# Order of work in a mixture of experts: gathers ahead of scatters, routing steps a tile apart, a last weight copy to another place, and twelve unread products

## What is computed

```python
x = _layernorm(x + _L0_attn_ref(x, ...))          # gated linear attention
x = _layernorm(x + _L0_xattn_ref(x, ctx_768, ...)) # 16 heads, 77 context rows
x = _layernorm(x + _L0_ffn_ref(x, ...))            # 8 experts, the best 2 of each token
x = _layernorm(x + _L1_attn_ref(x, ...))
x = _layernorm(x + _L1_xattn_ref(x, ctx_768, ...))
x = _layernorm(x + _L1_ffn_ref(x, ...))

def _L0_ffn_ref(x, Wg, W1, W2, W3):
    ...
    for e in range(E):
        u = jnp.einsum('bsd,dh->bsh', x, W1[e])
        v = jnp.einsum('bsd,dh->bsh', x, W2[e])
        h = u * jax.nn.sigmoid(u) * v
        y = jnp.einsum('bsh,hd->bsd', h, W3[e])
        out = out + y * weights[..., e][..., None]
```

## Time and profile before

| | us |
|---|---|
| median of 3 runs | 1141.53 |
| lowest and highest run | 1140.96, 1144.29 |
| the profiled execution, whole | 1150.01 |
| its span, first to last instruction | 1148.3 |
| PE busy in it | 1013.1 (88%) |
| DVE, ACT, POOL busy | 617.3, 425.2, 255.9 |
| mean granted clock of PE, of its full speed | 0.968 |

### The profile page before, as it was taken

The page is one execution under the profiler, slowest core; times in us unless marked ns, Lnnn a source line. Parts: engine busy times, 40 slices in busy tenths (PEclk is TensorE's granted clock), DMA queues, the critical chain, the costliest instruction groups (busy, mean ns, idle before and its releaser), DMA issues.

```text
span 1148.3 us, 20834 instructions
## 1 busy us (share of the span) xinstructions
PE 1013.1 (88%) x8628; PEld 723.1 (63%) x8628; DVE 617.3 (54%) x1398; ACT 425.2 (37%) x557; POOL 255.9 (22%) x282
## 2 busy tenths in 40 slices
PE   6889889889998898999998798989888987986887
PEld 3666566566565798997445465756556574753656
DVE  2653753753867463333334845665574759755333
ACT  1533533533513445555541244152406323340212
POOL 0310310310210223333332130231103111202642
PEclk9999999999988898999999899999999999997999
DMA  6014313213201971111112000200010010005427
GB/s 186 1 42 149 109 42 125 69 42 121 73 1 32 370 237 37 47 47 47 47 43 92 1 5 2 83 2 6 16 59 2 6 37 1 2 1 152 151 88 233
DMA packets 64238, 80.50 MB, mean 70 GB/s; under 512 B 12736, under 2 KB 57681, under 8 KB 63121
## 3 DMA queue, kind: packets, MB, share of 16 engines
q1 hardware_dynamic: 53392, 61.15, 16.1%
q0 software_dynamic: 5664, 15.47, 4.2%
q10 hardware_dynamic: 5088, 2.56, 0.9%
HBM read 46.13 MB, written 33.03 MB: 69 GB/s over the span
## 4 chain that ended last, share of the span: by engine, by line
PE 44%; issue 21%; DVE 16%; ACT 12%; SPq 2%; DMA 2%; POOL 2%; another core or an unknown queue 1%; ACTq 0%; DVEq 0%; POOLq 0%
PE ps L1511 8%; DVE sb_arena L865 6%; ACT sb_arena L642 6%; PE ps L1647 5%; PE ps L1669 3%; PE ps L1717 3%; PE ps L1772 3%; DVE sb_arena L869 3%; PE ps L1619 2%; PE ps L1983 2%; DVE ps L886 2%; PE ps L1555 1%; SPq L433 1%; PE ps L1998 1%
## 5 line engine op out<-in xcount | busy, mean ns | idle before, releaser
L642 ACT ACTIVATE sb_arena<-ps 77x2048 f32<-77x2048 f32 (+1 forms) x64 | 116.7, 1880 | 28.2 <-PE ps L1601 27.0
L1377 POOL TENSOR_TENSOR sb_arena<-sb_arena,sb_neghalf 128x2 f32<-128x2 f32 x40 | 28.7, 719 | 398.1 <-DVE sb_arena L831 398.1
L1511 PE MATMUL ps<-sb_arena,sb_wreg 128*128 128x256 f32 (+1 forms) x512 | 109.0, 361 | 6.8 <-issue 3.8
L1846 PE MATMUL ps<-sb_arena 128*128 128x128 f32 x800 | 104.4, 287 | 2.4 <-ACT sb_arena L750 2.1
L1846 PEld LDWEIGHTS ps<-sb_arena 128*128 128x128 f32 x800 | 101.2, 203 | 4.5 <-ACT sb_arena L750 2.8
L1511 PEld LDWEIGHTS ps<-sb_arena,sb_wreg 128*128 128x128 f32 (+1 forms) x512 | 88.0, 193 | 23.3 <-issue 8.3
L1619 PE MATMUL ps<-sb_arena 32*77 32x256 f32 (+1 forms) x1024 | 79.4, 428 | 25.3 <-ACT sb_arena L642 12.7
L750 ACT ACTIVATE sb_arena<-sb_arena 128x1024 f32 x72 | 76.0, 1056 | 17.1 <-issue 13.1
L1619 PEld LDWEIGHTS ps<-sb_arena 32*77 32x77 f32 (+1 forms) x1024 | 45.0, 179 | 45.8 <-ACT sb_arena L642 23.7
L865 DVE TENSOR_REDUCE sb_arena<-ps 128x8 f32<-128x2048 f32 x32 | 71.1, 2285 | 3.5 <-PE ps L1575 3.5
L1452 POOL DMA_INDIRECT outs<-sb_arena,sb_idx x36 | 36.3, 1010 | 145.6 <-ACT sb_arena L740 145.6
(11 more groups left out here) (285 smaller groups left out, 1890.4 us busy)
## 6 DMA issues: line engine op xcount, KB each, us to landing
sb_arena<-in_m_w SPq DMA_DIRECT2D x8, 1536.0 KB, 10.7
sent<-sb_xres SPq DMA_DIRECT2D x32, 256.0 KB
sb_arena<-outs SPq DMA_DIRECT2D x16, 512.0 KB, 6.3
outs<-sb_zeros SPq DMA_DIRECT2D x4, 1664.0 KB, 9.8
sent<-sb_zeros SPq DMA_DIRECT2D x2, 2560.0 KB, 13.7
sb_arena<-in_m_w SPq DMA_DIRECT2D x16, 256.0 KB
early<-sb_xres SPq DMA_DIRECT2D x12, 256.0 KB, 2.9
sb_arena<-in_xT SPq DMA_DIRECT2D x8, 256.0 KB, 3.4
```

Of the source, the lines that this page charges most:

```text
L642: nc.scalar.activation(dst, src, ACT.Exp).then_inc(S(f"h_PT{p}"), 1)
L1511: ins = mm(dst[:, m * cols:(m + 1) * cols], wt[0:rows, k, m * P:(m + 1) * P], src[0:rows, k, 0:cols], start=(k == 0), stop=(k == KC - 1))
L1846: ins = mm(to[:, m * P:(m + 1) * P], w[:, k, m * P:(m + 1) * P], slots0[j % 2].xT[:, k, :], start=(k == 0), stop=(k == KC - 1))
```

## The change

It has five parts.

1. In POOL's loop the gather of tile `j + 4` stands ahead of the scatter of tile `j`.
2. The steps of the late placement move: ACT's copy of the table comes at the end of its turn 7 in place of 8, PE's `place_late` in turn 5 in place of 4, DVE's `index` after tile 9 in place of 8, and the routing weights at tile 10 in place of 9 on ACT and DVE.
3. The third weight matrix of the last tile (35) goes to the place of the first matrix, whose last reader is the u of that tile, and ACT copies it ahead of the output of tile 34. The last output product reads it there.
4. In the last pair of the first layer, six unread products stand ahead of the first key product of each member, twelve in all.
5. The helper `weights_of` takes both offsets, which serves part 3.

The diff, cut to its core (the calls in `hidden_halves` and `weights_of` change only in the added argument):

```diff
@@ -52,8 +52,9 @@
-LATE_CHOOSE, LATE_RANK, LATE_HOTS, LATE_TABLE, LATE_QUANTA, LATE_RAW, LATE_INDEX, LATE_WEIGHTS = 0, 2, 3, 5, 6, 8, 8, 9
+LATE_CHOOSE, LATE_RANK, LATE_HOTS, LATE_TABLE, LATE_QUANTA, LATE_RAW, LATE_INDEX, LATE_WEIGHTS = 0, 2, 3, 5, 6, 8, 9, 10
 FAR = 128 * P
+IDLE_LAST = 6
@@ -741,14 +742,17 @@
             def weights0(j, part, used, signal):
 
+                last = j + 1 == TILES0 and part == 2
                 if j < E:
                     act.wait_ge(S(f"landed{j}"), 16)
-                if j:
+                if last:
+                    act.wait_ge(S("t_u"), TILES0)
+                elif j:
                     act.wait_ge(S(used), j)
                 act.wait_ge(S("table"), 4 if j >= WHOLE0 else 3 if j >= SURE else 2)
                 blk = act.value_load(copied_of(j), min_val=0, max_val=max(BLOCKS))
-                nc.scalar.activation(arena[:, WORDS * WORK + 1024 * part:WORDS * WORK + 1024 * (part + 1)],
-                                     arena[:, bass.ds(blk * WORDS + 1024 * part, 1024)], ACT.Copy).then_inc(S(signal), 1)
+                to = WORDS * WORK + (0 if last else 1024 * part)
+                nc.scalar.activation(arena[:, to:to + 1024], arena[:, bass.ds(blk * WORDS + 1024 * part, 1024)], ACT.Copy).then_inc(S(signal), 1)
@@ -757,10 +761,13 @@
                 gate0(j)
                 if j + 1 < TILES0:
                     weights0(j + 1, 0, "t_u", "t_c1")
+                if j + 1 == TILES0:
+                    weights0(j, 2, "t_y", "t_c3")
                 if j:
                     outputs0(j - 1)
+                if 0 < j < TILES0 - 1:
                     weights0(j, 2, "t_y", "t_c3")
-                if j == LATE_RAW:
+                if j == LATE_RAW - 1:
                     picks(2, 2)
                 if j == LATE_WEIGHTS:
                     router(1)
@@ -1448,12 +1455,12 @@
             for j in range(TILES0):
+                if j + XBUFS < TILES0:
+                    gather0(j + XBUFS)
                 pool.wait_ge(S("t_ys"), j + 1)
                 g.indirect_dma_start(outs0[:, :], bass.IndirectOffsetOnAxis(ap=idx0[:, j:j + 1], axis=0), y0t[j % XBUFS], None
                                      ).then_inc(S(f"t_out{j % XBUFS}"), 16)
-                if j + XBUFS < TILES0:
-                    gather0(j + XBUFS)
-                else:
+                if j + XBUFS >= TILES0:
                     unread(j % XBUFS)
@@ -1606,6 +1613,8 @@
                 b, kz = bufs[p], keys_of(c, p)
+                if c is X0 and n + 1 == PAIRS and u == 0:
+                    idle(p, IDLE_LAST)
                 if u == 0:
                     pe.wait_ge(S(f"h_nmT{p}"), c.at(n) + 1)
@@ -1884,13 +1893,14 @@
             def output_halves(j, blk):
                 p = j % 2
+                at = 0 if j + 1 == TILES0 else 2 * KC * FH
...
-                        ins = mm(bank(1, 3)[rows, 0:D], slots0[p].hT[:, m, rows], weights_of(c, blk, 2 * KC * FH + D * m, D), start=(m == 0),
+                        ins = mm(bank(1, 3)[rows, 0:D], slots0[p].hT[:, m, rows], weights_of(c, blk, 2 * KC * FH + D * m, D, at + D * m), start=(m == 0),
@@ -1909,7 +1919,7 @@
-                if j == LATE_HOTS + 1:
+                if j == LATE_HOTS + 2:
                     place_late(0)
```

More of the change, by code:

```diff
@@ L1873, in hidden_halves @@
                         rows = slice(QROWS * c, QROWS * (c + 1))
-                        ins = mm(to[rows, :], slots0[j % 2].xT[:, k, rows], weights_of(c, blk, at + FH * k, FH), start=(k == 0), stop=(k == KC - 1),
+                        ins = mm(to[rows, :], slots0[j % 2].xT[:, k, rows], weights_of(c, blk, at + FH * k, FH, at + FH * k), start=(k == 0), stop=(k == KC - 1),
                                  skip_group_check=True)
```

4 lines of the change are left out of this document (2 added, 2 removed).

## The result

| | before | after |
|---|---|---|
| median of 11 runs each, us | 1143.87 | 1136.44 |
| lowest and highest run | 1140.96, 1145.82 | 1133.47, 1140.81 |
| the profiled execution, whole | 1150.01 | 1135.14 |
| its span | 1148.3 | 1133.3 |
| mean granted clock in it | 0.968 | 0.977 |

The account below looks back on a forecast made before the run. PE was taken to work nearly without a break, losing time to a few waits and slow-clock products. Terms 5.0 + 0 + 5.5 + 1.0 + 0.2 = 11.7 us, so 1141.5 to 1129.8 us, range 1126.8 to 1134.7.

Parts of the forecast that it names:

- the last one of the sum: Level: the 11.7 us gain taken over unchanged from the profiled execution to the median, 1141.5 to 1129.8 us.
- table a turn sooner: Tiles 8 to 10: ACT's earlier table copy removes the sorting's wait and slow products; 5.5 us, bounds 3 and 5.8.
- gathers first: Tiles 3 to 5: gathers ahead of scatters remove the wait for rows and slow products; 5.0 us, bounds 3 and 5.3.
- last weight copy: End of the mixture: the last output product no longer waits for ACT's weight copy; 1.0 us, bounds 0.7 and 1.1.
- twelve unread products: Last pair's key products: unbroken work brings the full clock back; 0.2 us, bounds -2.3 and 0.4.
- DVE takes over: v of tile 5 to u of tile 8: DVE's chain sets the time, PE waits about 1.1 us; gain 0.
- A: Last pair: unread products paid at the low clock without bringing it back in time; 2.4 us worse, 1132.2; chance 0.17.
- B: Tiles 3 to 5: another wait takes PE's lead; at worst 4.9 us come back, 1134.7; chance 0.10.
- C: Tile 8: the new 1.1 us wait, or a similar one, lowers the clock once; 2.9 us, 1132.7; chance 0.06.
- D: Mixture: the slow products do not hang on the waits and stay; 4.4 us less gain, 1134.2; chance 0.03.
- E: Tile 8: the sorting still waits, for the place table or DVE; 5.5 us stay, 1135.3; chance 0.02.
- F: Second layer: clock falls in more places, 2.9 us each, making it slower than before; 1147.2 with six; chance 0.02.

Follow-up runs that it names:

- again: The kernel before once more, with no edit; median 1146.01 us over 12 runs, ratio 0.999.
- look1: One more traced execution of the kernel before, with no edit; it took 1149.98 us.
- look2: A further traced execution of the kernel before, with no edit; it took 1152.81 us.
- part4: The kernel before with only the twelve unread products added in the last pair; ratio 0.9982.
- fill: The kernel before with nine unread products ahead of the sorting, filling the wait for the copied table; ratio 0.9996.
- part1: The kernel before with only the gathers put ahead of the scatters; median 1143.64 us, ratio 0.9977.
- no4: The changed kernel without the twelve unread products; median 1139.78 us, ratio 0.9904 to before.
- part2: The kernel before with only the late placement steps moved; ratio 0.9968.
- after_again: The changed kernel once more, with no edit; median 1138.04 us, ratio 0.9901 to before.
- look3: One more traced execution of the changed kernel, with no edit; it took 1137.87 us.
- router_end: The changed kernel with the routing weights moved behind the last tile; median 1136.64 us, ratio 0.9893 to before.
- best: The changed kernel with routing weights behind the last tile and the placement steps from the second owner table on one tile later; median 1135.57 us, ratio 0.9883.

## Why the prediction missed

**The step that failed first is the last one of the sum.** "The profiled execution is 8.5 us above the median, spread over the whole of it as far as I can see, so I take the difference over unchanged" fixed the level by a median of three runs, 1141.53, and took one execution for a usual one. More runs put the median of before at 1143.87, so 2.3 of the 6.6 us were there before any term of the change; with that level the forecast is 1132.2, and a range moved along with it would end at 1137.0 and hold the measured 1136.44. The later sets of before ran at 1147.21, 1148.87 and 1148.31, each beside another set of experiments. The 8.5 us do not look like an overhead of profiling: the profiled execution of after, 1135.14, is below its own median, and later runs of before reach 1155.74. The runs of one set of before lie 5 to 16 us apart. The sets differ too: the highest run of the first, 1145.82, lies below the median of each later one, so scatter within a set does not explain the level, and what does is open. Neither three runs nor a trace carries the level to 1 us.

The range of 7.9 us had no part for this, and it was narrower than its own terms. Their gains add up to 4.1 us at the low bounds and 12.9 at the high ones, which is 1128.6 to 1137.4 and not the "1127.5 to 1131.5" that the prediction gives as coming from them. The measured 1136.44 lies within the first.

**The second step that failed is a term:** the table a turn sooner, put at 5.5 us, measured 3.9.

**The terms**, by the traces that have the edit against those that have not:

| term | forecast | measured | from |
|---|---|---|---|
| gathers first, u3 to u8 | 5.0 | 4.7 | 29.19 against a mean of 33.9 (before, again, look1, look2, part4, fill) |
| table a turn sooner, u8 to u10 | 5.5 | 3.9 | 11.77 against a mean of 15.65 (before, again, look1, look2, part1, part4) |
| last weight copy | 1.0 | 0.87 | 152.69 against 153.56 |
| twelve unread products | 0.2 | about 0.2, unsure | scores to first transposition, like with like (5. below); by plain means 1.1: 6 traces with, 35.2, 8 without, 36.3 |
| sum | 11.7 | 9.7 | |

9.7 us lie inside the measured 9.0 (7.1 to 11.1), and inside the 11.4 (7.7 to 15.1) of the second comparison. Four of the six traces behind the first two means are executions of 1150 to 1153 us, slower than any median of before, so these means may be too high: the other two alone give 4.0 in place of 4.7 (part4, fill) and 3.1 in place of 3.9 (part1, part4). The single parts add up as well: 2.6, 3.7 and 2.1 us by their ratios and 0.87 for part 3, which was not run alone, are 9.3, though two of the three intervals include nothing gained. That something is given back behind the mixture is neither shown nor ruled out: from the last output to the end of the span it is 544.8 us on average in eight traces without the last weight copy's new place, and 545.9 in the four of the changed kernel and no4. Each kind scatters by some 3 us around that (541.4 to 548.8 and 541.7 to 549.6), so a loss of 1 or 2 us would not be seen.

1. **Gathers first: right.** 13.04 us was foretold for u of tile 3 to v of tile 5, and 13.04 is what every trace of the changed kernel shows, without a wait. With the old order the loss is not always at tile 4: the longest wait is at tile 7 in again, where v5 to u8 took 19.17, and in part2, look1 and fill it is shared by tiles 4, 5 and 7. Only the sum over the stretch says what the order of issue costs.
2. **DVE takes over: right.** 16.15 from v5 to u8 for 16.08, and a wait of 0.93 for the forecast 1.1. But the gain of nothing held for the one trace at hand. In again and part2 the old order lost time here too, at tile 7 (19.17 and 17.10 us). Over the six traces the gathers bring 4.1 us up to v5 and 0.6 behind it.
3. **Table a turn sooner: right mechanism, term too large.** 11.74 was foretold and 11.77 came. But the term was sized by the one trace of before in which the clock stayed low for longest: of 17.22 us, 3.15 were the slow clock. In the other traces it is 1.6 or, in part4, nothing. The 2.0 of the wait is certain; the share of the clock was sized from one execution. This makes the term 1.6 us too large.
4. **Last weight copy: right**, 0.87 for 1.0, and 0.83 us from the start of DVE's copy to the product (590.81 to 591.64) for the 0.75 foretold.
5. **Unread products: right where the prediction looked; elsewhere only estimated.** What decides this stretch is the clock behind the wait of 1.53 us ahead of member 1's scores, before any of the twelve products. The work ahead of that wait is the same in all 14 traces, yet there are three outcomes, and within each the traces with and without the twelve products can be compared. The figures are scores to values, then scores to first transposition:
   - The clock is low from the scores on (2.00 us for them): 15.41 and 37.2 with (after_again), 15.61 to 15.80 and 36.9 to 37.4 without (before, look1, look2, fill).
   - It falls during or right behind the scores: 13.79 and 35.4 with (look3), 14.61, 15.12 and 36.1, 36.8 without (again, part2).
   - It stays full (1.13 us): 12.25 and 34.4 to 34.8 with (part4, after, router_end, best), 12.51, 12.50 and 34.7, 34.4 without (part1, no4). Here the products cover a wait of 2.02 us behind which part1 and no4 have slow key products, a case that the prediction did not work out, but up to the first transposition that saves nothing.

   The gains up to the first transposition are -0.2, 1.1 and 0.0 us; weighted by how often each outcome came (5, 3 and 6 of 14), this is 0.2 us, an estimate, since two of the outcomes have a single trace with the products. The plain means give 1.1 because four of the six traces with the products, and two of the eight without, happened to have the full clock. That is luck of the draw. Why the same wait of 1.53 us has three outcomes stays open.

**The rivals.** A (paid at the low clock) did not happen: 1.15 us key products in after_again. B did not: no other wait took the lead of tiles 3 to 5. C did not: the waits of 0.93 and 0.91 us leave the following rows at 2.02 and 2.05. D, that the slow products do not hang on the waits, does not fit this stretch: in all seven traces whose table comes a turn sooner and in fill nothing slow follows the sorting, while five of six with the wait have 3.3 to 3.8 us. The Trainium skill, page "TensorE: Matmul & The Clock Gate", section "HAM oscillation — how this bites in real kernels", which would have let a gap of this length pass, is not borne out by these rows. But "the clock falls behind a wait of 2.0 us" is a tendency, not a law: part4 is the exception, and fill shows less than it seems, since part4 reached the same without filling. E did not happen. F (slower than before) did not either.

**The account of the 6.6 us.** 2.3 are the level of before. The medians of before and after differ by 7.4 us where 11.7 were forecast, which is the other 4.3: 2.0 are the terms (11.7 less 9.7), of which 1.6 are the table's, 0.7 lie between the terms and the 9.0 us of the ratio, inside its interval, and 1.6 between that ratio and the difference of the two medians. For the last two pieces no cause is shown; the scatter of the runs is large enough for both. That the same two kernels gave 9.0 and then 11.4 us belongs there too, since the intervals overlap.

## What to carry to other kernels

Waits whose causes lie within the engines came out as forecast to within 0.2 us, but waits for transfers, and what the clock loses behind any wait, differ from execution to execution, so size such a term from several traces of the same kernel, not from the one at hand. Take the level from many runs, let the range hold the scatter of the base beside the bounds of the terms, and add these bounds up. When traces are averaged, first sort them by what happened ahead of the edit. Where a queue issues both fetches that somebody waits for and results that nobody waits for, issue the fetches first: here the results' later issue cost nothing, and the waits that it removed were of another size in each run.

## What the runs showed of the hardware

- Executions of one kernel on one core differ by over 1% (1138.43 to 1154.2 us in 12 runs of the kernel before), and the mean granted clock follows the time (0.981 to 0.961). Within each of the timed kernels the correlation of time and clock is -0.7 to -0.97, with 0.5 to 0.9 us for each 0.001.
- From tile 3 on, the row of products behind PE's waits of 0.73 to 1.53 us took its usual 1.95 to 2.05 us. Behind waits of 1.97, 2.41 and 2.51 us for rows it took 3.27, 3.45 and 3.20, but behind one of 2.55 us 1.95 (part4). Behind the one of 2.02 us it took 3.3 to 3.8 in five traces and 2.05 in one. So the length of the last wait alone does not say whether the clock falls.
- One wait of 1.53 us in the last pair, with the same rows ahead of it in all 14 traces, was followed by the low clock at once in five, by a fall within the next row or right behind it in three, and by the full clock in six (the scores behind it took 2.00, 1.16 to 1.35, and 1.13 us).
- The mixture starts at the low clock in all 14 traces, whichever kernel: tile 0's u takes 3.75 to 3.79 us in place of 1.95, behind waits of 0.70 to 1.56. In before the granted clock is 0.50 from 378 to 384, and PE had been busy for 1.29 and 1.61 of 2.00 us in the two windows from 374 to 378. The change leaves this loss in place.
- At the low clock (1.2 of 2.4 GHz) six unread products took 2.74 us in place of 1.47, and the key products behind them took 1.15 us at once.
- In the old order of issue gathered rows kept PE waiting 0.73 to 2.55 us at tiles 4, 5 and 7, the longest time at tile 4 in five traces and at tile 7 in two. In before the DMA engines' busy share was 0.99 to 1.07 from 385 to 420, with the weight loads under way.

The rows behind two of these points, which no section above shows: the scores behind the wait of 1.53 us in before (beside the 1.13 us of after at 344.41), and tile 0's u there (PE):

```profile
340.52 2.01 PE L1580 MATMUL ps<-sb_arena 32*128 32x77 f32 x32 [1.53 <-DVE sb_arena L869]
...
379.19 3.79 PE L1846 MATMUL ps<-sb_arena 128*128 128x128 f32 x16 [1.23 <-ACT sb_arena L750]
```
